# Three attentions of a fused eight-layer kernel: GpSimd splits the row maxima and normalises, and one copy of x is issued later

## The reference, cut to what matters

```python
x = x + L0_xattn(_layernorm(x), ctx, ctx)   # attention A0, 16 heads of 8
x = x + L0_ffn(_layernorm(x))               # 8 experts, top 2
x = x + L1_xattn(_layernorm(x), ctx)        # attention A1, rotary q and k
x = x + L1_ffn(_layernorm(x))               # quantised
x = x + L2_xattn(_layernorm(x), ctx, ctx)   # attention A2, one k/v head shared
x = x + L2_ffn(_layernorm(x)); x = x + L3_xattn(_layernorm(x), ctx); x = x + L3_ffn(_layernorm(x))
```

## Time and profile before

| | us |
|---|---|
| median of three runs | 1466.83 |
| the profiled execution, as timed | 1466.42 |
| its span in the profile | 1464.6 |
| A0, first scores to last add_x | 29 to 226 |
| A1, the same | 560 to 780 |
| A2, the same | 860 to 1034 |
| busy share: PE, DVE, ACT, POOL | 81%, 68%, 46%, 37% |

### The profile page before, as it was taken

One profiled execution on the slowest core, in us unless ns is written; L12 is line 12 of the kernel. 1 busy time (PEld: TensorE's weight loads), 2 busy tenths in 40 slices (PEclk: granted clock), 3 DMA queues, 4 the chain that ended last, 5 costly groups with the idle time before them and its releaser, 6 DMA issues. The chain is left out here.

```text
span 1464.6 us, 34924 instructions
## 1 busy us (share of the span) xinstructions
PE 1180.8 (81%) x11141; PEld 925.2 (63%) x11154; DVE 990.4 (68%) x2918; ACT 666.8 (46%) x1423; POOL 538.4 (37%) x590
## 2 busy tenths in 40 slices
PE   4799994349999957789987879999799966499991
PEld 2577773338899815566663456677477756399991
DVE  4599886564533247989974678888487777766552
ACT  2467771116555403345554546766234343144440
POOL 3223303674325166534411232431121125752554
PEclk9899996559999957889998989999799977599996
DMA  7787733012233267435532177564200042133552
GB/s 187 197 206 189 186 106 130 30 53 74 86 89 109 66 153 190 118 101 150 144 84 51 43 176 174 145 162 106 87 1 0 0 152 74 53 120 106 147 143 73
DMA packets 140294, 163.33 MB, mean 112 GB/s; under 512 B 15240, under 2 KB 120734, under 8 KB 133196
## 3 DMA queue, kind: packets, MB, share of 16 engines
q1 hardware_dynamic: 131980, 145.38, 37.3%
q0 software_dynamic: 8192, 16.46, 4.1%
HBM read 111.19 MB, written 50.92 MB: 111 GB/s over the span
## 5 line engine op out<-in xcount | busy, mean ns | idle before, releaser
L604 DVE TENSOR_REDUCE A_neg_max<-A_s_bank 128x4 f32<-128x512 f32 x384 | 253.5, 687 | 54.6 <-PE A_s_bank L747 44.2
L464 ACT ACTIVATE A_probsT<-A_st_bank 128x512 f32<-128x512 f32 x384 | 222.2, 602 | 44.4 <-PE A_st_bank L760 43.2
L747 PE MATMUL A_s_bank<-A_k_stack,A_q_stack 72*128 72x128 bf16 x1536 | 159.4, 230 | 40.6 <-DVE A_neg_max L604 23.4
L760 PE MATMUL A_st_bank<-A_q_stack,A_k_stack 128*128 128x128 bf16 x1536 | 154.0, 225 | 7.2 <-DVE A_q_stack L620 6.2
L760 PEld LDWEIGHTS A_st_bank<-A_q_stack,A_k_stack 128*128 128x128 bf16 x1536 | 113.4, 104 | 53.2 <-issue 43.1
L747 PEld LDWEIGHTS A_s_bank<-A_k_stack,A_q_stack 72*128 72x128 bf16 x1536 | 107.4, 102 | 55.6 <-DVE A_neg_max L604 33.7
L772 PE MATMUL A_pv_bank<-A_probsT,A_v_pad 128*32 128x128 f32 x3072 | 128.1, 285 | 0.7 <-issue 0.7
L2065 ACT ACTIVATE E_h<-E_h_bank,w_L_b 128x256 f32<-128x256 f32 x184 | 76.5, 471 | 72.7 <-PE E_h_bank L2165 71.7
L2177 PE MATMUL E_y_bank<-E_w,E_h 128*128 x736 | 90.4, 276 | 2.2 <-ACT E_h L2065 0.9
L772 PEld LDWEIGHTS A_pv_bank<-A_probsT,A_v_pad 128*32 128x32 f32 x3072 | 74.4, 111 | 24.2 <-issue 2.6
L2165 PE MATMUL E_h_bank<-E_xT,E_w_u 128*128 128x256 f32 x368 | 88.6, 385 | 0.0
(11 more groups left out here) (369 smaller groups left out, 2652.1 us busy)
## 6 DMA issues: line engine op xcount, KB each, us to landing
A_q_stack<-q_scratch SPq DMA_DIRECT2D x48, 576.0 KB
A_k_stack<-k_scratch SPq DMA_DIRECT2D x32, 576.0 KB
q_scratch<-A_q_parts SPq DMA_DIRECT2D x48, 192.0 KB, 2.3
A_k_stack<-k_scratch SPq DMA_DIRECT2D x48, 192.0 KB
E_xe<-slots_in SPq DMA_DIRECT2D x53, 128.0 KB, 2.0
slots_out<-E_ye SPq DMA_DIRECT2D x53, 128.0 KB, 1.7
A_ctxT<-in_ctxT SPq DMA_DIRECT2D x24, 256.0 KB, 9.4
k_scratch<-A_k_parts SPq DMA_DIRECT2D x32, 192.0 KB
```

Of the source, the lines that this page charges most:

```text
L464: act.activation(probsT[n % 2][:, c * HQ:(c + 1) * HQ, :], st_bank[c % 2][:, :].rearrange("k (a q) -> k a q", a=HQ), ACT.Exp, scale=scale) ...
L604: dve.tensor_reduce(neg_max[:, c * HQ:(c + 1) * HQ], s_bank[c % 2][:, :].rearrange("q (a k) -> q a k", a=HQ), AX.X, ALU.max, negate=True). ...
L747: last = pe.matmul(s_bank[c % 2][:, a * S:(a + 1) * S], q_stack[slot][0:COMBO, h, at:at + S], k_stack[slot][0:COMBO, h, at:at + S], start= ...
L760: last = pe.matmul(dst, k_stack[slot][:, h, at:at + S], q_stack[slot][:, h, at:at + S], start=True, stop=spread)
```

## The change

- `split_max` is a function of the engine. DVE runs it for entries 0 and 1; after that POOL does, once per entry (in A1 from entry 8 on; until then DVE does). `neg_max` has two buffers, and `row_max` of piece 0 waits on DVE for the split of two entries before.
- POOL normalises groups 2 and later (in A1 group 4 and later), and DVE only the earlier ones. `statistics` on DVE waits for `xn_done`, that is for the normalisation of the group before, since both use the same `mv` and `rstd`.
- POOL's program is ordered by entries: in entry b it splits the maxima of b+2, then adds the bias (entry 0 of a group, A2 only), does split_rest of k (entry 1), of q (entry 2), or the inverse deviation and normalisation of group g+3 (entry 3).
- A1 takes statistics three groups ahead, as A0 and A2 do; its DVE program has one round more outside the loop, and POOL has no loop any more.
- SP issues the third part of x after `prep(1)`.

```diff
-    if rope:
-        NORM_AHEAD = 2
-        STATISTICS, NORMALISE = {0: range(GB)}, {2: range(GB)}
-    else:
-        NORM_AHEAD = 3
-        STATISTICS, NORMALISE = {0: range(0, 2), 2: range(2, GB)}, {6: range(0, 2), 7: range(2, GB)}
+    NORM_AHEAD = 3
+    STATISTICS = {0: range(0, 2), 2: range(2, GB)}
+    POOL_FIRST = 2 * GB if late else 0
...
-        neg_max = sb("neg_max", [S, NH], F32)
+        neg_max = [sb(f"neg_max{i}", [S, NH], F32) for i in range(2)]
...
             prep(0)
             constants(2)
+            constants(3)
+            prep(1)
             if begin:
                 begin.load_x(sp, 2)
-            constants(3)
-            prep(1)
...
+        def split_max(eng, own, b, n):
+
+            eng.wait_ge(max_done, 4 * (b + 1))
+            if not (isinstance(b, int) and b == 0):
+                eng.wait_ge(mt_ready, b)
+            core.settle(eng)
+            own.link(eng.tensor_copy(max_parts[:, hi:hi + NH], neg_max[n % 2][:, :]))
+            core.settle(eng)
+            eng.tensor_tensor(max_parts[:, lo:lo + NH], neg_max[n % 2][:, :], max_parts[:, hi:hi + NH], ALU.subtract)\
+                .then_inc(m_split, 1)
+            eng.wait_ge(m_split, b + 1)
...
+            def normalise(g):
+
+                inverse_deviation(g)
+                pool.wait_ge(rstd_done, g + 1)
+                pool.wait_ge(prep_ready, U * (g - 1) + X + 1)
+                for j in range(GB):
+                    last = pool.tensor_scalar(xn[:, j, :], core.x_tile(g * GB + j), mv[:, j, 0:1],
+                                              rstd[:, j:j + 1], ALU.subtract, ALU.mult)
+                last.then_inc(xn_done, 1)
...
+            add_bias(0)
+            normalise(4 if late else 2)
+            for b in range(POOL_FIRST, NB):
+                g = b // GB
+                if has_scores(b + 2):
+                    split_max(pool, own, b + 2, b)
+                if b % GB == 0 and exists(g + 1):
+                    add_bias(g + 1)
+                if b % GB == 1 and exists(g + 2):
+                    split_rest(pool, own, k_f, k_parts, kd, g + 2, KL, k_lead, k_split)
+                if b % GB == 2 and exists(g + 2):
+                    split_rest(pool, own, q_f, q_parts, D, g + 2, QL, q_lead, q_split)
+                if b % GB == 3 and exists(g + 3):
+                    normalise(g + 3)
...
             def statistics(at, tiles=range(GB)):
 
+                if tiles[0] == 0 and not (isinstance(at, int) and at < 2):
+                    dve.wait_ge(xn_done, at)
...
-            def row_max(b, c):
+            def row_max(b, n, c):
+                if c == 0 and not (isinstance(b, int) and b < 2):
+                    dve.wait_ge(m_split, b - 1)
...
-                    if has_scores(b + 2):
-                        split_max(b + 2)
+                    if isinstance(b, int) and b < POOL_FIRST:
+                        split_max(dve, own, b + 2, n)
```

More of the change, by code:

```diff
@@ L118, in multi_head_attention @@
     QL, KL = (Q2, K2) if rope else (Q1, K1)
-    dve_steps = 2 * (GB * 2 + GB)
+    dve_steps = 2 * (GB + GB)
     CREDIT = 2
@@ L564, in statistics, with normalise @@
                     last.then_inc(stats_done, 1)
[L566 to L574, removed]
+            def normalise(g):
+                dve.wait_ge(rstd_done, g + 1)
+                dve.wait_ge(stats_done, g + 1)
+                if g > 0:
+                    dve.wait_ge(prep_ready, U * (g - 1) + X + 1)
+                for j in range(GB):
+                    last = dve.tensor_scalar(xn[:, j, :], core.x_tile(g * GB + j), mv[:, j, 0:1],
                                              rstd[:, j:j + 1], ALU.subtract, ALU.mult)
-                if tiles[-1] == GB - 1:
-                    last.then_inc(xn_done, 1)
+                last.then_inc(xn_done, 1)
             def rotate(g, use, dst, parts, split, written, copies, lead):
@@ L600, in prep @@
                     rotate(g, use, q_f, q_parts, q_split, qw_done, 2, q_lead)
-            def row_max(b, c):
+            def row_max(b, n, c):
+                if c == 0 and not (isinstance(b, int) and b < 2):
+                    dve.wait_ge(m_split, b - 1)
                 dve.wait_ge(s_ready, 4 * b + c + 1)
-                dve.tensor_reduce(neg_max[:, c * HQ:(c + 1) * HQ], s_bank[c % 2][:, :].rearrange(
+                dve.tensor_reduce(neg_max[n % 2][:, c * HQ:(c + 1) * HQ], s_bank[c % 2][:, :].rearrange(
                     "q (a k) -> q a k", a=HQ), AX.X, ALU.max, negate=True).then_inc(max_done, 1)
[L607 to L615, removed]
             def spread_max(b, n):
@@ L648, in between @@
                     if g == 4:
-                        normalise(0, 0)
+                        normalise(0)
                     if g == 5:
@@ L653, in between @@
                         prep(V, 0, 0)
-                        normalise(1, 1)
+                        normalise(1)
                 layer.dve(dve, between)
@@ L660, in _ @@
                 statistics(g)
-                normalise(g, g)
+                normalise(g)
                 for use in range(U - g):
@@ L669, in _ @@
                 for c in range(4):
-                    row_max(b, c)
-                split_max(b)
+                    row_max(b, b, c)
+                split_max(dve, own, b, b)
             if spread:
                 spread_max(0, 0)
-            if NORM_AHEAD == 3:
+            if not late:
                 statistics(2)
-                normalise(2, 2)
             def late_result(i):
@@ L693, in place @@
                             dve.wait_ge(begin.x_loaded[2], 16)
-                        if at in STATISTICS and exists(ahead):
+                        if late and isinstance(it, int) and it == 0:
+                            if at == 0:
+                                statistics(n // GB + 2)
+                            elif at == 2:
+                                normalise(n // GB + 2)
+                            elif (n, at) == (7, 6):
+                                statistics(4)
+                        elif at in STATISTICS and exists(ahead):
                             statistics(ahead, STATISTICS[at])
-                        if at in NORMALISE and exists(ahead):
-                            normalise(ahead, ahead, NORMALISE[at])
                         for use, g in uses_at(at, it * 2 + n // GB):
@@ L702, in entries @@
                     if has_scores(b + 2):
-                        row_max(b + 2, 0)
-                        row_max(b + 2, 1)
+                        row_max(b + 2, n, 0)
+                        row_max(b + 2, n, 1)
                     divide(b)
```

4 lines of the change are left out of this document (2 added, 2 removed).

## The result

The changed kernel takes 1505.47 us (median of four runs, 1499.8 to 1508.74), the kernel before 1466.11 us beside it: ratio 1.0271 (95% interval 1.025 to 1.0292), 39 us slower, where 1463 with a range to 1477 was forecast. The profiled execution has a span of 1502.9 us, 38.3 more than before. Lines have moved: row_max is L619, the POOL split L335 and L337, transpose_max L790, spread_max L625, add_x L643, the normalisation on POOL L398, the statistics on DVE L573.

The account below looks back on a forecast made before the run. A 4.66 us loop per plain entry, PE's work then DVE's row maximum and divide, was taken as the bound. Sum: 1466.4 - 4.9 (x) + 2.5 (A0) - 3.1 (A1) + 2.5 (A2) = 1463.4 us, range 1442 to 1477.

Parts of the forecast that it names:

- The loop over PE, 4.66 us, without DVE's split: Plain entries: PE from L792 to scores 1, 3.39 us, then DVE row maximum and divide, 1.27; period stays at 4.66.
- Rival A: DVE's sum of work binds and its wait for POOL hides; 24 us less, 1442 us; chance 0.30.
- The split on POOL, done at T+0.83 against T+0.86: Each entry, T ending its fourth row maximum: POOL's split ready at T+0.83, PE needs it at T+0.86, so no loss.
- Rival B: POOL's split comes after T+0.86 in every entry, delaying L781 and the whole loop; +16 us, 1479; chance 0.17.
- The length of the normalising instruction: POOL's four 128x128 normalising instructions at a group's end: 0.33 us each, 1.3 in all.
- The wait: DVE's statistics at a group's end wait for POOL's normalisation, ending T3+3.6: 1.0 us (0.5 to 2.1).
- How many: Waits of DVE's statistics on POOL of about 1 us: four in A0 and four in A2.
- What a wait costs: Net +0.75 us a group for four groups each in A0 and A2: +3.0 in each.
- A1, forecast -3.1: A1, entries 8 to 22: stalls against DVE's freed time, 84.8 us where it was 87.95, so -3.1.
- rival C: Stacks come late in A0 or A2 because q's split ends later; 4 us, 1467; chance 0.08.
- The x copies, -4.9: Third part of x copied later frees the full DMA queue early in A0: -4.9 us, bounds 0 and -8.2.
- Rival D: The move of the x copies doesn't help; 1468 us; chance 0.07.

Follow-up runs that it names:

- the forms above: Changed kernel with POOL's four normalising instructions in four forms (immediates, 64 columns, subtract only, original), normalised x wrong by intention; 1496.28 us in a single run.
- with two buffers: Changed kernel with two buffers each of mv and rstd, so statistics wait for the normalisation of two groups before; 1466.11 us, ratio 1.0004 to the kernel before.

## Why the prediction was wrong, step by step

- **The loop over PE, 4.66 us, without DVE's split**: right. In plain entries of the changed kernel L801 (L792 before) stands at 200.65 and 205.31, again 4.66 us, and the difference of the add_x stays at 10.0 from entry 23 to 31. Rival A (1442) fell with it: DVE is busy for 35 us less (955.6 for 990.4) and nothing got shorter. The 0.5 us for the six plain entries of an attention was nothing.
- **The split on POOL, done at T+0.83 against T+0.86**: right, with 0.20 and 0.22 us measured for the 0.21 assumed and T+0.79 in the timeline above. Rival B's place was right but not its price: PE's weight load waits for the split for 18.7 us in all, 11.5 of it in A1, where the longer split_rest stands ahead of the split, and only 2.6 us in A0 in 5 of its 30 entries.
- **The length of the normalising instruction**: this is the term that failed. Taken 0.33 us, with ends 0.20 and 0.61; measured 0.78, over the 0.5 that the prediction gave as a sign of being wrong. It was sized as the cast of the earlier trace rows by its columns, but a column costs 3.4 ns here and 0.8 there, and an empty instruction 0.36 for the 0.2 assumed; leaving out the second operation or the numbers per row takes only 0.19 or 0.14 off (the forms above). The two ends were rows of other kinds of instruction, and the upper one was no bound. The Trainium skill (GPSIMD Engine Reference, 3.1 Elementwise) gives 1.96 times DVE's time for a two-input add, and the prediction set it aside because this instruction has one input; the estimate by it was 2.35 us for four. The trace has 3.13, 2.6 times the 1.2 us of the earlier trace rows, so the estimate was too low as well, but it erred on the right side.
- **The wait**: its place, its chain and DVE's arrival were right (T3+2.6 forecast and measured). POOL ends at T3+5.6 for T3+3.6, 1.8 us of that by the instruction. So it was 3.2 us for 1.0, above the bound of 2.1. (The forecast's own terms add to T3+3.53, not T3+3.6.) With 2.2 us more in each of the eight places and 2.0 in each of A1's two, and nothing else changed, the forecast's sum would be about 1485 us: by this estimate the one term is half of the miss of 42 us.
- **How many**: eight forecast in A0 and A2, ten measured. The statistics of group 3 wait for the normalisation of group 2 as well, which POOL does too; I counted from group 4. These two are 0.4 and 2.3 us; the eight of the loops are 3.0 to 3.3.
- **What a wait costs**: forecast as its length less what was free, 0.75 a group; measured 2.9 to 3.9 in A0, of which 0.3 is there with two buffers too. Of the 2 to 3 us between, the longer wait is 2.2. The rest I put to the clock: L790 stands at T0+1.14 instead of T0+0.85 (T0 is the end of the next entry's last row maximum), the next row maximum waits 0.6 longer, and the two entries behind lose up to 1.0 and 1.1; with two buffers they lose up to 0.8 and 0.15. No run changed the clock by itself. The prediction didn't ask what PE's clock does once PE stands for 2.5 us. A group of A2 loses more (4.8 to 5.7) for waits of the same length: PE stands 2.6 to 2.9 us there for 2.3 to 2.6, and the lower clock lasts longer (0.50 to 0.63 for 0.72). That this is the whole difference is not shown.
- **A1, forecast -3.1**: wrong in sign. From entry 8 to 22 it is +8.6. Two waits for A_xn, forecast at 1.15 each, are 3.1; the split of T3, forecast at T3+2.2, is done at 698.97, T3+2.7. What is left of A1's waits when DVE splits (4.1 and 2.9 us) shows that POOL's q split alone makes it late there. They cost less than their length: from entry 8 to 22 that kernel is at +7.5, and with two buffers at +3.0, 4.5 us for 7.1. And even with the wait gone (two buffers, split on POOL) the same stretch is at +2.5; at +3.0, with the split gone too, the stacks come late by 2.6 us at most: rival C's mechanism, in the one attention where I had not looked for it. In no run did DVE's relief show as a gain there.
- **The x copies, -4.9**: right in the trace (-4.2 for the first stack, -5.8 by entry 2), -2 to -3 in the medians. It is part of every kernel here that starts from the changed one. Rival D is out in the traces and not quite in the medians.
- **The rivals**: the one that came true was none of the four but the end of my own case, beyond its bound. The slower case that I named had its place in the split; the true one had its place in the normalisation, and I had written down the 8 us that the Trainium skill's factor would make, without giving it a chance. One bound was also miscounted: a stall of 0.5 in eight places and -8.2 for x make 1456, not 1453.

The accounts: the wait and what hangs on it is 39.4 us (changed kernel 1505.5, two buffers 1466.1), and that is shown. What is left of the change, 0.0004 above before, is the x copies (-2 to -3 by 0.9981 and 0.9984) and some +3 for the split on POOL and the new order of its program; this second part is a difference between intervals that overlap.

## What to carry to other kernels

A step moved to an idle engine needs the duration of its own form there, from a row or from a small run; here the row of a simpler form with four times the columns (0.61 us) was not an upper bound for it (0.80 us). Where an edit hands a buffer from one engine to the other, look who writes it next: here one pair of small buffers, doubled, was worth 39 us. And ask what TensorE's clock does behind a wait: in A0 and A2 stops of 2.3 to 2.9 us all had the lower level behind them and stops of 0.7 to 1.3 us two times in eight, and halving the waits gave back over 60% of what they cost.

## What the runs showed that I had not expected

POOL's tensor_scalar with two numbers per row takes 0.36 us and 3.4 ns for each of 128 columns, slower for 128 columns (0.80 us) than its plain cast of 512 (0.61 us).

DVE's copy into the q stack is held up by POOL's two-input passes: 1.69 us for 0.69 where they meet, here in the changed kernel.

```profile
141.12 1.69 DVE L625 COPY A_q_stack<-A_max_rows 32x2048 bf16<-32x2048 bf16 x1
```

```profile
141.09 1.16 POOL L325 TENSOR_TENSOR A_k_parts<-A_split_r,A_k_parts 128x512 bf16<-128x512 f32 x1 [0.18 <-POOL A_k_parts L323]
```

It starts with POOL's pass and ends 0.56 us behind it. In A0 of the changed kernel the copy meets a two-input pass seven times and takes 1.09 to 1.69 us, and each time it ends 0.55 to 0.56 us behind POOL's end, however long the two overlap. The Trainium skill (SBUF — State Buffer, Who interferes with whom) has the one block the other for a whole instruction, and the trace agrees: nearly all of DVE's 0.69 us come when POOL's 1.16 are over. What the rule hits is spread_max, a place that the prediction had not named, and there it cost nothing that could be measured. The prediction used the rule to say that the normalisation stays undisturbed beside the row maxima. The traces agree: POOL's instruction takes 0.79 to 0.81 us beside them. But the one of the four that meets spread_max is held up, to 1.14 us in the changed kernel, where that happens once in A0 from 80 to 200 us, and to 1.14 to 1.31 us with two buffers, where it happens in every group. That is why its mean in this stretch is 909 ns there and 819 in the changed kernel. Its mean with two buffers, and one such meeting:

```profile
L400 POOL TENSOR_SCALAR A_xn<-x_sb,A_mv,A_rstd 128x128 f32<-128x128 f32 x16 | 14.4, 909 | 0.4
73.78 1.30 POOL L400 TENSOR_SCALAR A_xn<-x_sb,A_mv,A_rstd 128x128 f32<-128x128 f32 x1
73.86 0.71 DVE L629 COPY A_q_stack<-A_max_rows 32x2048 bf16<-32x2048 bf16 x1
```
